# The sums of attention's value products in 64x64 tiles of TensorE, over two PSUM banks

## What is computed

```python
def _L1_ffn_ref(src, in_proj_w, in_proj_b, out_w, out_b, gate_w, gate_b, w1, b1, w2, b2, ...):
    s_len, bsz, d = src.shape            # 8, 256, 256
    qkv = src @ in_proj_w.T + in_proj_b
    q, k, v = jnp.split(qkv, 3, axis=-1)           # each reshaped to (s_len, bsz, H, dh)
    scores = jnp.einsum('sbhd,tbhd->bhst', q, k) * dh ** (-0.5)
    attn = jax.nn.softmax(scores, axis=-1)
    ctx = jnp.einsum('bhst,tbhd->sbhd', attn, v).reshape(s_len, bsz, d)
    attn_out = ctx @ out_w.T + out_b
    x = _ln(src + attn_out, ln1_g, ln1_b)
    logits = x.reshape(-1, d) @ gate_w.T + gate_b   # then the best 2 of 8 experts of each row
    ...
```

## Time and profile before

| | |
|---|---|
| median of 3 runs | 1131.95 us (1131.2 to 1134.01) |
| the profiled execution, its own time | 1130.92 us |
| its span in the trace | 1129.2 us |
| PE busy in the span | 1065.4 us (94%) |
| DVE, ACT, POOL busy | 748.4 (66%), 467.6 (41%), 521.4 us (46%) |
| granted TensorE clock, mean | 0.992 |
| chain that ended last, by engine | PE 63%, DVE 18%, POOL 5%, ACT 4% |
| of that chain, line 2381 / line 2370 | 3% / 2% |
| line 2381, PE | 512 records, 61.1 us busy |

### The profile page before, as it was taken

The page is one execution under the profiler, slowest core; times in us unless marked ns, Lnnn a source line. Parts: engine busy times, 40 slices in busy tenths (PEclk is TensorE's granted clock), DMA queues, the critical chain, the costliest instruction groups (busy, mean ns, idle before and its releaser), DMA issues.

```text
span 1129.2 us, 22086 instructions
## 1 busy us (share of the span) xinstructions
PE 1065.4 (94%) x7978; PEld 871.2 (77%) x7978; DVE 748.4 (66%) x1698; ACT 467.6 (41%) x938; POOL 521.4 (46%) x511
## 2 busy tenths in 40 slices
PE   9999989988899999999889999999999989989997
PEld 6788756666788667999768999999998678875664
DVE  5899789999887448889742222222223998987784
ACT  2554677765555202121112222222222456653466
POOL 5645235568773214768664110100363757531342
PEclk9999999999999999999979999999999999999999
DMA  6999900002000300000147141211221200000001
GB/s 218 367 405 388 350 2 2 26 1 90 1 1 1 106 0 1 1 11 29 52 151 303 57 184 38 107 37 37 75 70 44 61 11 10 2 1 1 1 28 47
DMA packets 45129, 93.66 MB, mean 83 GB/s; under 512 B 3933, under 2 KB 19070, under 8 KB 42486
## 3 DMA queue, kind: packets, MB, share of 16 engines
q1 hardware_dynamic: 36646, 62.24, 15.5%
q0 software_dynamic: 7104, 29.14, 7.2%
q10 hardware_dynamic: 1296, 1.18, 0.3%
HBM read 39.02 MB, written 51.51 MB: 80 GB/s over the span
## 4 chain that ended last, share of the span: by engine, by line
PE 63%; DVE 18%; issue 6%; POOL 5%; ACT 4%; DMA 2%; POOLq 1%; PEldq 0%; DVEq 0%; another core or an unknown queue 0%; ACTq 0%; SPq 0%; PEld 0%
PE PS L2516 10%; PE PS L2526 10%; PE PS L1109 6%; PE PS L2025 4%; PE PS L2381 3%; PE PS L1122 3%; PE PS L1087 3%; PE PS L1077 2%; PE PS L2370 2%; PE PS L1904 2%; PE PS L1739 2%; POOL big L695 2%; PE PS L1035 1%; DMA expert_out<-scr 1%; DVE big L1410 1%
## 5 line engine op out<-in xcount | busy, mean ns | idle before, releaser
L2550 ACT ACTIVATE scr<-PS,W 128x128 f32<-128x128 f32 x148 | 53.5, 367 | 193.4 <-PE PS L2516 192.3
L2516 PEld LDWEIGHTS PS<-scr 128*128 128x128 f32 x992 | 116.4, 192 | 6.8 <-issue 3.2
L2516 PE MATMUL PS<-scr 128*128 128x128 f32 x992 | 118.6, 276 | 2.9 <-issue 1.5
L2526 PE MATMUL PS<-scr 128*128 128x256 f32 x496 | 112.2, 379 | 0.0
L2581 DVE TENSOR_SCALAR scr<-PS,W 128x128 f32<-128x128 f32 x148 | 51.3, 351 | 85.2 <-PE PS L2516 85.2
L727 POOL TENSOR_TENSOR scr<-scr,small 128x1232 f32<-128x1232 f32 x32 | 72.0, 2250 | 73.3 <-DVE small L478 73.1
L868 ACT ACTIVATE big<-PS 128x512 f32<-128x512 f32 x144 | 73.0, 523 | 69.0 <-PE PS L1087 67.7
L2587 DVE TENSOR_TENSOR scr<-PS,W 128x256 f32<-128x256 f32 x37 | 15.7, 425 | 128.2 <-PE PS L2526 118.9
L2526 PEld LDWEIGHTS PS<-scr 128*128 128x128 f32 x496 | 91.8, 190 | 11.2
L2627 POOL DMA_DIRECT2D expert_out<-scr x28 | 15.2, 544 | 161.0 <-DVE scr L2587 157.0
L1109 PEld LDWEIGHTS PS<-scr,big 128*128 128x128 f32 x640 | 81.0, 191 | 8.1 <-issue 5.1
(11 more groups left out here) (426 smaller groups left out, 2451.2 us busy)
## 6 DMA issues: line engine op xcount, KB each, us to landing
expert_in<-zeros SPq DMA_DIRECT2D x1, 19712.0 KB, 59.7
expert_out<-zeros SPq DMA_DIRECT2D x1, 19712.0 KB, 111.8
scr<-ew_in POOLq DMA_DIRECT2D x12, 1024.0 KB, 6.3
scr<-expert_in SPq DMA_DIRECT2D x38, 128.0 KB
big<-ew_in POOLq DMA_DIRECT2D x4, 1024.0 KB, 9.0
expert_out<-scr POOLq DMA_DIRECT2D x28, 128.0 KB, 2.0
W<-pack SPq DMA_DIRECT2D x1, 2458.0 KB, 9.1
W<-pack SPq DMA_DIRECT2D x1, 2152.0 KB, 8.9
```

Source lines behind the costliest of these rows:

```text
L2516: ins = pe.matmul(bank(1 + f % 4, G), e_w1[slot][:, k, f * P:(f + 1) * P], e_xT[:, k, :], start=(k == 0), stop=(k == C - 1))
L2526: ins = pe.matmul(bank(5 + t, D), e_h[:, f, t * P:(t + 1) * P], e_w2[slot][:, f, :], start=(f == 0), stop=(f == FC - 1))
```

## The change

`values_summed` cuts each of its 128x128 matmuls into four of 64x64: rows `r` (64 positions) by columns `k` (64 features). A half of the positions gives only its own half of the turned columns, so it is multiplied with the 64x64 diagonal block of the identity. The two halves of rows write different banks, 4 and 5, from word 256 on. Each unit then has 64 matmuls of 64 columns, before 16 of 128. ACT's copy reads both banks in one instruction, still 128x256.

Bank 5 is shared now, so other things move: products_summed goes to bank 7, turned to bank 5, and PE waits for `cT_ready` (ACT's copy of the unit before) ahead of turned instead of after it. The residual matmul is split off as `based` and moves ahead of that wait, with the wait for `y_taken`; in the iterations with `ranked` it stays where it was. The wait for `bias_taken` moves ahead of the loop.

```diff
+        SUM_BANKS, SUM_AT = (4, 5), 256
...
-                    raw = bank(5, H * B).rearrange("p (t h) -> p h t", h=H)
+                    raw = bank(7, H * B).rearrange("p (t h) -> p h t", h=H)
...
-                    a.activation(s_cT[u % 2], bank(4, D).rearrange("p (c n) -> p c n", c=C), ACT.Copy).then_inc(s["cT_ready"], 1)
+                    sums = PS[:, SUM_BANKS[0]:SUM_BANKS[1] + 1, SUM_AT:SUM_AT + P]
+                    a.activation(s_cT[u % 2].rearrange("p c (r n) -> p c r n", r=2), sums.rearrange("p r (c n) -> p c r n", c=C),
+                                 ACT.Copy).then_inc(s["cT_ready"], 1)
...
+                half = P // 2
                 for c in range(C):
                     for t in range(B):
-                        ins = pe.matmul(bank(4, P, c * P), vp[:, t, c * P:(c + 1) * P], ident, start=(t == 0), stop=(t == B - 1))
+                        for r in range(2):
+                            rows = slice(r * half, (r + 1) * half)
+                            for k in range(2):
+                                at = c * P + k * half
+                                ins = pe.matmul(PS[k * half:(k + 1) * half, SUM_BANKS[r], SUM_AT + c * half:SUM_AT + (c + 1) * half],
+                                                vp[rows, t, at:at + half], ident[rows, rows], start=(t == 0), stop=(t == B - 1))
...
+            def based(u):
+                pe.matmul(bank(6, D), ident, m_Z[:, tile_of(u), :], start=True, stop=False)
+
             def projected(u):
-                pe.matmul(bank(6, D), ident, m_Z[:, tile_of(u), :], start=True, stop=False)
-                pe.wait_ge(s["cT_ready"], u + 1)
...
+                if it:
+                    if turns(TAKES, it - 1):
+                        pe.wait_ge(s["y_taken"], turns(TAKES, it - 1))
+                    if u < UNITS:
+                        if q is None:
+                            based(u)
+                        pe.wait_ge(s["cT_ready"], u + 1)
                 if q is not None and it < UNITS:
                     pe.wait_ge(s["xT_ready"], x)
-                    clocked(pe, 7, 9)
+                    clocked(pe, 5, 9)
                 if 0 <= x < UNITS:
                     turned(x)
```

More of the change, by code:

```diff
@@ L2340, in samp_act @@
                     a.wait_ge(s["d_psum"], u + 1)
-                    a.activation(s_cT[u % 2], bank(4, D).rearrange("p (c n) -> p c n", c=C), ACT.Copy).then_inc(s["cT_ready"], 1)
+                    sums = PS[:, SUM_BANKS[0]:SUM_BANKS[1] + 1, SUM_AT:SUM_AT + P]
+                    a.activation(s_cT[u % 2].rearrange("p c (r n) -> p c r n", r=2), sums.rearrange("p r (c n) -> p c r n", c=C),
+                                 ACT.Copy).then_inc(s["cT_ready"], 1)
                 if 0 <= x < UNITS:
                     a.wait_ge(s["xT_psum"], x + 1)
-                    a.activation(s_xT[x % 2], bank(7, D).rearrange("p (c n) -> p c n", c=C), ACT.Copy).then_inc(s["xT_ready"], 1)
+                    a.activation(s_xT[x % 2], bank(5, D).rearrange("p (c n) -> p c n", c=C), ACT.Copy).then_inc(s["xT_ready"], 1)
                 if it + 1 == B:
@@ L2369, in products_summed @@
                 for d in range(DH):
-                    ins = pe.matmul(bank(5, H * B), ident, prod[:, d, :], start=(d == 0), stop=(d == DH - 1))
+                    ins = pe.matmul(bank(7, H * B), ident, prod[:, d, :], start=(d == 0), stop=(d == DH - 1))
                 ins.then_inc(s["b_pe"], 1)
@@ L2388, in turned @@
                 for c in range(C):
-                    ins = pe.transpose(bank(7, P, c * P), m_X1[:, tile_of(u), c * P:(c + 1) * P], ident)
+                    ins = pe.transpose(bank(5, P, c * P), m_X1[:, tile_of(u), c * P:(c + 1) * P], ident)
                 ins.then_inc(s["xT_psum"], 1)
@@ L2428, in samp_pe @@
             clocked(pe, 4, 16)
+            pe.wait_ge(bias_taken, EARLY_BIAS)
             for it in range(LAST + 1):
                 u, x, q = it - 1, it - 3, batch_at(it, 4)
+                if it:
[5 more added lines that the diff above has]
+                        pe.wait_ge(s["cT_ready"], u + 1)
                 if q is not None and it < UNITS:
                     pe.wait_ge(s["xT_ready"], x)
-                    clocked(pe, 7, 9)
+                    clocked(pe, 5, 9)
                 if 0 <= x < UNITS:
@@ L2445, in samp_pe @@
                     if 0 <= u < UNITS:
+                        if q is not None:
+                            based(u)
                         ins = projected(u)
```

4 lines of the change are left out of this document (removed).

## The result

The changed kernel takes 1138.07 us (median of 6 runs, 1137.09 to 1143.75) against 1134.27 us of the kernel before in the same session: recorded ratio of the runs 1.0048, 95% interval 1.0026 to 1.0069 (the quotient of the two medians is 1.0034). The forecast was 1126.8 us with a range to 1133.5, 5.2 us faster than before; the kernel is slower, so the sign is wrong too. The kernel before itself measured 2.3 us above the median that the forecast started from, which explains none of the sign. The profiled execution has a span of 1135.4 us, 6.2 more than before.

The account below looks back on a forecast made before the run. PE was taken to bound samp until 502 us, PE and POOL together afterwards, with little overlap after 553. Gains of 4.1 + 0 + 1.1 = 5.2 us from 1131.95 gave 1126.8 us, range 1124.8 to 1133.5.

Parts of the forecast that it names:

- A unit's sums: PE's values_summed for one unit: 2.05 us after the change, 1.5 us less than the 3.57 before.
- the upper bound: For a unit's sums: 32 ns per record, the shortest over a longer run in the trace, giving 4.2 us a unit.
- rivals 1 and 2: PE issue limits: sums hardly faster, 1131.5 to 1134 us, chance 0.14; or slower, 1145 us at 32 ns, chance 0.12.
- First stretch: samp from 437 to 502 us, where DVE waits for PE: 4.1 us gained, bounds 3.0 to 4.9.
- The loop: Dependency loop through POOL, PE and DVE in the first stretch, setting a pair of units at 13.2 us.
- Second stretch: samp from 502 to 553 us, where PE and POOL run neck and neck: 0 gained, bounds 0 and 1.3 us.
- Rival 3: Clock falls in new PE gaps, second stretch: 1.5 to 2 us lost each, about 1130 us with two, chance 0.14.
- The end: After 553 us: last sums 1.5 us shorter, less 0.4 for transposes now after the copy; 1.1 us gained.
- the few tenths for each packet: PE's instruction fetch: if about 10 to 12 more packets each showed for this, 2 to 3 us would go.
- What follows samp I expect shifted as a whole: Everything after samp moves earlier unchanged; the first load of moe comes at about 580.7 instead of 585.92 us.
- Three things were named as what would make it wrong: Unit sums of 3 us or more, samp's clock at 0.50 before 560 us, or samp's earlier end not moving moe.
- the rule weighed before: Trainium skill's fixed matmul overhead of about 60 cycles: 25 ns per record, 3.2 us a unit, nearly nothing gained.

Follow-up runs that it names:

- e2: Changed kernel with bf16 filler matmuls into bank 7 where PE waits long (unit 1, iterations 9, 13, 15 to 18); median 1137.45 us.
- e7: Changed kernel with tiled sums for units 0 to 7 only, plus 6 filler products ahead of unit 1's sums; median 1130.80 us, ratio to before 0.9970.
- e3: Changed kernel with tiled sums for units 0 to 7 only, units 8 to 15 untiled; median 1130.91 us, ratio to before 0.9977.
- e9: Changed kernel, all sums tiled, POOL's scatters of units 9 and 10 moved behind the next stage's first weights load; ratio to before 1.0014.
- e10: Changed kernel with units 0 to 7 and 15 tiled, 6 fillers ahead of unit 1, scatters of units 9 and 10 moved later; ratio to before 0.9990.
- e4: Changed kernel with 64 short filler matmuls in place of 16 ahead of unit 0, shifting the instruction fetch; one profiled run, no total time given.
- e1: Changed kernel with the old untiled 128x128 sums, moved banks and order kept; ratio to before 1.0012, with 1 in its interval.
- e5: Changed kernel with tiled sums for units 0 to 14, the last unit's untiled; ratio to before 0.9997.
- e6: Changed kernel with only the last unit's sums tiled, units 0 to 14 untiled; ratio to before 1.0051.

## Why the prediction was wrong, by its own steps

- **A unit's sums, 2.05 us: right** (2.09). The old unit was read a little short, 3.57 us, where those of the pair it adds up take 3.67 on the chain. A matmul record starts every 16 ns, half of the 32 ns that was the upper bound, so rivals 1 and 2 are excluded.
- **First stretch, 4.1 us (3.0 to 4.9): nearly right.** 3.8, with one clock fall in it that costs 1.0; 4.8 without (e2, e7). POOL then takes back 1.2 us (column to 558 of e2, e3, e7), so that some 3.6 us stay. DVE's waits fell to 2.0 us and not to 1. The loop was read rightly: two of POOL's products, a pair of units apart, start at 465.16 and 478.10 us, 12.9 us (forecast 13.2; before 14.7).
- **Second stretch, 0 ("a loss has no source as long as the sums get shorter"): wrong by 2.2.** 1.2 us are that give-back and 1.0 the clock fall at 508.7, after the wait of 2.80 us for POOL. In e7 POOL's product at 500.68 (504.33 before) is 3.75 us early, counted from unit 0. DVE's values of unit 9 are 4.82 us early, those of unit 10 only 3.77: POOL is next in line there. The source of the clock fall was that the sums get shorter. Rival 3 had named this fall and its place, and priced it at 1.5 to 2 us; it measured 1.0. It foresaw neither the fall in unit 1 nor that falls alone would not turn the sign.
- **The end, +1.1 us: this step failed.** It measured -2.6, 3.7 us from the forecast, the largest error of the sum. The arithmetic was not at fault: without scatters beside the sums the tiled last unit does gain 1.5 us against before (e9, e10). What failed is that the term took the last unit's result as ready when its sums end, and put the extra instructions at nothing ("hidden as long as the sums do not outrun the fetch"). It had no term for what POOL issues at that moment. With POOL's scatters beside it, the tiled burst pauses and its increment comes 2.0 to 3.4 us after the last record: 4.1 us, from -1.5 in e9 to +2.6. Waiting for instructions does stop the sums, as far as e4 shows, in units 4, 8 and 12 for 1.3 to 1.6 us. I had counted packets over the whole span (12 more, as came: `q8 instruction: 64`) and not asked what a single packet does to a burst. But these pauses cost next to nothing in the table, since PE had slack there. So neither the few tenths for each packet nor the 2 to 3 us in all describe what happened.
- **"What follows samp I expect shifted as a whole": wrong by 2.8.** The stretch to 586 us lost 1.2 us, as it did with untiled sums (e1 +1.1), so the tiles are not needed for it; e3 has the same order and +0.1. Behind 586 us 1.6 more were lost. At 1034.4 us the clock stood at 0.50 for 6.8 us, where before it was 3.4 at 1031.8. It is no matter of the tiles: e1, e5 and e7 have 6.8 there, e3 and e9 3.4. How much of the 1.6 it cost is open. The six traces with 6.8 lost 1.2 to 3.9 us behind 586, the four others with 3.4 between -0.7 and +0.7, but e4 and e6, with no fall there, 0.7 and 1.7.
- **The start** gave 2.5 us more in this execution, and between 0.1 and 2.6 in the others: an execution's own. With it the profile's 6.2 us is 2.5 - 3.8 + 2.2 + 2.6 + 1.2 + 1.6, to rounding; the medians differ by 3.8 us, and 0.48% would be 5.4.
- **The signs.** Three things were named as what would make it wrong. The sums did not take 3 us or more at full clock. The clock did show 0.50 before 560 us, at 447.3. That the earlier end of samp would not move moe was not put to the test, since samp ended later.

What stays open is the inside of the late increment. That tiled sums and POOL's scatters must meet at the last unit is shown; how scatters hold up PE is not. That it goes through the instruction fetch would fit, but two things speak against a packet as its condition. Unit 14 pauses without one. And an increment 2.2 to 2.4 us late stands at about 552 us too, in the kernel before as well (DVE waits 2.08 us there on "remote"), behind four untiled matmuls of 8 columns and during the six scatters. Timeline of DVE, of the kernel before:

```profile
554.38 0.20 DVE L2207 TENSOR_TENSOR scr<-scr,PS 128x48 f32<-128x48 f32 x1 [2.08 <-remote]
```

In e7 the same wait is 2.26 us, at 550.89, and no packet of q8 is under way from 545.4 to 564.8. So scatters can delay a semaphore of PE with neither tiles nor a packet, and why the untiled last sums escape it is not known. Nor is it known why the stretch to 586 us costs 1.1 us in e1 and 0.1 in e3.

## What to carry to other kernels

Count the instructions that a faster form puts into a burst, not over the span. Here a burst as long as a packet of instructions (256) stopped for 1.3 to 1.6 us in three units of 16, which cost nothing where PE had slack. Look also at what other engines issue beside the burst that lies bare on the path: here indirect DMAs of POOL turned its gain of 1.5 us into a loss of 2.6. Use the fast form only in the stretch whose bound it lifts; here 8 units of 16 gave the whole gain, and the one unit that lay bare on the path gave it back. A waiting engine that becomes faster leaves gaps, and the clock charged about 1 us for each of two here; six products into a free bank in the gap repaid one (e7), but fillers issued once the clock was down cost time (e2).

## What the runs showed of the hardware

- 128 loads and 128 matmuls of 64x64 tiles issue in 2.09 us, 16 ns from matmul to matmul, 65 ns for a group of four with the changes of tiling counted in (forecast 2.05 us, 64 ns). The Trainium skill (TensorEngine Tiling (Array Packing), Instruction Overhead), the rule weighed before, would have each matmul hold 60 cycles, by an estimate 25 ns at 2.4 GHz; this trace does not agree.
- PE's instructions come in packets of 16384 bytes, 256 to a packet, 0.9 to 1.6 us each. Where a tiled burst ran dry in the kernel after the loads went on 1.4 to 1.6 us after the packet's end (469.85 to 471.37, 499.38 to 500.98).
- Beside POOL's scatters a tiled burst paused three times for 0.5 to 0.7 us with no packet near (unit 14). Without scatters the last unit's burst ran through in 2.10 us (e9), and untiled sums ran through beside them (e5).
- A semaphore increment can come 2.0 (kernel after), 2.75 (e6) and 3.4 us (e4) after the modelled end of the matmul that carries it, with scatters beside it each time. ACT's idle time ended by "remote" was the only mark of it in the views; the copy's start against the last sum's end shows it.
